# Raw expert weights loaded into the place of their f16 parts, and the expert's number loaded first in the expert step

## The reference

```
xn = layernorm(x)
x  = x + differential_attention(xn) + moe(xn)

def moe(xt):                       # 8 experts, 2 of them for each token, and a shared expert for all
    logits = xt @ gate_w.T
    idx    = top_k(logits + beta, 2);  probs = sigmoid(logits[idx])
    h      = silu(xt @ gate_proj_w[e]) * (xt @ up_proj_w[e])       # 256 -> 512
    out    = sum over the token's two experts of probs * (h @ down_proj_w[e])
    return out + shared_expert(xt)
```

## Time and profile before

| | us |
|---|---|
| median of 3 runs | 3512.49 (3509.45 to 3520.72) |
| the profiled execution, whole | 3520.69 |
| its span in the profile | 3518.9 |
| TensorE busy in the span | 3220.9 (92%) |
| VectorE busy | 2810.6 (80%) |
| ScalarE busy | 2318.1 (66%) |
| POOL busy | 1648.7 (47%) |

### The profile page before, as it was taken

How to read it: one execution, slowest core, us unless ns; L and a number is a source line. 1 busy time by engine, 2 the same in 40 slices (tenths; PEclk the granted TensorE clock), 3 DMA queues, 4 the chain that set the end, 5 groups by cost and what they waited for, 6 DMA issues and landing times. The chain is left out here.

```text
span 3518.9 us, 61065 instructions
## 1 busy us (share of the span) xinstructions
PE 3220.9 (92%) x19800; PEld 1295.5 (37%) x19815; DVE 2810.6 (80%) x4905; ACT 2318.1 (66%) x3660; POOL 1648.7 (47%) x2104
## 2 busy tenths in 40 slices
PE   6777789999999999999999999868999999999987
PEld 3434456663222222222222222252333333333333
DVE  5564643468999999999999999476888999889997
ACT  3342333335888888788888878856767767777763
POOL 1331340002444444434344444405777888888885
PEclk9887899998999999999999999988999999999998
DMA  3233221111111111111111111041222222222221
GB/s 126 95 102 97 99 74 55 54 49 44 31 50 39 39 38 36 35 35 35 35 32 34 30 30 31 17 156 52 70 72 65 75 82 70 73 81 69 73 75 52
DMA packets 160888, 211.62 MB, mean 60 GB/s; under 512 B 32324, under 2 KB 108364, under 8 KB 160604
## 3 DMA queue, kind: packets, MB, share of 16 engines
q1 hardware_dynamic: 141340, 172.51, 16.4%
q0 software_dynamic: 8512, 18.76, 1.7%
q10 hardware_dynamic: 10752, 16.78, 1.4%
HBM read 154.48 MB, written 52.69 MB: 59 GB/s over the span
## 5 line engine op out<-in xcount | busy, mean ns | idle before, releaser
L1408 ACT ACTIVATE prob<-psS 128x1024 f32<-128x1024 f32 (+3 forms) x1280 | 1104.4, 906 | 278.9 <-PE psS L1592 269.4
L1458 DVE TENSOR_REDUCE pmax<-psR 128x1 f32<-128x512 f32 x1674 | 1057.0, 684 | 78.4 <-PE psR L1534 46.6
L2234 POOL TENSOR_TENSOR hc<-h_d,crep 128x512 f32<-128x512 f32 x512 | 646.9, 1271 | 189.8 <-DVE h_d L2463 139.6
L1534 PE MATMUL psR<-kslab,qslab 48*128 48x512 bf16 (+3 forms) x2480 | 652.5, 351 | 22.4 <-DVE pmax L1458 14.0
L1607 PE MATMUL psVo<-prob,vaug 128*32 128x512 f32 (+3 forms) x5120 | 629.8, 546 | 1.3 <-ACT ov L1412 0.6
L1592 PE MATMUL psS<-qslab,kslab 51*128 51x512 bf16 (+3 forms) x2560 | 533.3, 354 | 39.9 <-ACT prob L1408 23.0
L2463 DVE TENSOR_TENSOR_SCAN h_d<-a,state,psU 128x512 f32<-128x512 f32 x384 | 489.3, 1275 | 0.0
L1323 POOL TENSOR_SCALAR_AFFINE_SELECT prob<-prob 128x256 f32<-128x256 f32 (+1 forms) x512 | 213.4, 420 | 533.1 <-ACT prob L1408 533.1
L2453 DVE TENSOR_TENSOR psU<-dtx,psX 128x512 f32<-128x512 f32 x512 | 356.2, 696 | 92.7 <-PE psX L2613 42.8
L1534 PEld LDWEIGHTS psR<-kslab,qslab 48*128 48x128 bf16 x2480 | 187.2, 94 | 629.0 <-DVE pmax L1458 478.6
L2366 ACT ACTIVATE a<-dt,a_neg 128x512 f32<-128x512 f32 x512 | 366.9, 724 | 54.1 <-DVE h_d L2463 53.2
(11 more groups left out here) (347 smaller groups left out, 5260.8 us busy)
## 6 DMA issues: line engine op xcount, KB each, us to landing
crep<-c_rows_d SPq DMA_DIRECT2D x256, 256.0 KB, 3.1
x_e<-rows_d SPq DMA_DIRECT2D x72, 128.0 KB, 2.0
y_d<-y SPq DMA_DIRECT2D x72, 128.0 KB, 1.7
q_d<-parts SPq DMA_DIRECT2D x48, 128.0 KB, 2.3
k_d<-parts SPq DMA_DIRECT2D x48, 128.0 KB, 2.3
qslab<-q_d SPq DMA_DIRECT2D x60, 96.0 KB
kslab<-k_d SPq DMA_DIRECT2D x60, 96.0 KB
raw_w<-n_L_ffn_gate_proj_w_dram ACTq DMA_DIRECT2D x8, 512.0 KB, 3.8
```

Of the source, the lines that this page charges most:

```text
L1408: act.activation(prob[g % BUFS][:, :, off:BLK], psS[g % 2][:, :, off:BLK], ACT.Exp).then_inc(prob_ready, 1)
L1458: dve.tensor_reduce(into[:, lo:lo + (count - 1) * NEXT + 1:NEXT], psR[at % BANKS][:, 0:count * w].rearrange("p (n w) -> p n w", w=w), AX.X ...
L1534: ins = pe.matmul(dst[:, m * w:(m + 1) * w], qslab[u][rows, i * P:(i + 1) * P], kslab[u][rows, ch * BLK:ch * BLK + w], start=(m == 0), sto ...
L2234: pool.tensor_tensor(hc[:, g % CR], h[:, g % HR], crep[:, g // PAIR % SPR], ALU.mult).then_inc(hc_ready, 1)
```

## The change

Front: the two f16 parts of a matrix of one expert now lie side by side (`wg`, `wu`, `wd` in place of six tensors `wgh` to `wdl`), which is as much room as the raw f32 matrix needs, and the raw matrix is loaded there. Scaling goes from there to a buffer `scaled_w` (the size of the old `raw_w`, for one expert), the high part is a copy of it in f16 over the raw values, and POOL subtracts from the same buffer. Each f16 copy now signals, and each subtraction waits for its own copy; each scaling waits for the last expert's subtraction of the same matrix. The load of expert 1 is issued ahead of ScalarE's block 0, and at the end of block n that of expert n+2. The six ScalarE operations of a block lie in another order. The maximum is three operations of 1024 instead of one of 3072. Expert step on TensorE: the `value_load` of the expert's number comes first, ahead of the transposes of h; the transposes of the next tile's x lie between G and U (for tile 0 they stay ahead of all).

```diff
--- before.py
+++ after.py
@@ -151,8 +151,10 @@
         gate_rows = hT[0:E, 0, 0:D]
         y = sg[:].rearrange("p s (j d) -> p (s j) d", d=D)
         wsg, wsu, wsd = sb("wsg", [P, KD, M]), sb("wsu", [P, KD, M]), sb("wsd", [P, M // P, D])
-        raw = sb("raw_w", [P, 3, KD * M])
-        zeros = raw[:, 0, 0:D]
+        scaled = sb("scaled_w", [P, 3, KD * M])
+        zeros = scaled[:, 0, 0:D]
+        raw = [keep[name][:].rearrange("p e x m -> p (e x m)").bitcast(F32).rearrange("p (e m) -> p e m", e=E)
+               for name in ("wg", "wu", "wd")]
         wmax = sb("wmax", [P, 3])
         wmax_r = sb("wmax_r", [3, 1])
         diag_r = sb("diag_r", [3, 3])
@@ -198,7 +200,7 @@
         raw_in = sem("a_raw_in")
         wscale_step = sem("a_wscale_step")
         wmax_moved = sem("a_wmax_moved")
-        whigh_ready = sem("a_whigh_ready")
+        wsplit_step = sem("a_wsplit_step")
         wlow_ready = sem("a_wlow_ready")
 
         block = ctx.enter_context(nc.Block())
@@ -269,11 +271,10 @@
         def _(pool):
 
             def low_weights(e):
-                for w, low in enumerate((keep["wgl"], keep["wul"], keep["wdl"])):
-                    high = (keep["wgh"], keep["wuh"], keep["wdh"])[w]
-                    pool.wait_ge(whigh_ready, 3 * e + w + 1 + CREDIT)
-                    pool.tensor_tensor(low[:, e].rearrange("p k m -> p (k m)"), raw[:, w],
-                                       high[:, e].rearrange("p k m -> p (k m)"), ALU.subtract).then_inc(wlow_ready, 1)
+                for w, name in enumerate(("wg", "wu", "wd")):
+                    pool.wait_ge(wsplit_step, 6 * e + 2 * w + 2 + CREDIT)
+                    pool.tensor_tensor(keep[name][:, e, 1], scaled[:, w], keep[name][:, e, 0], ALU.subtract)\
+                        .then_inc(wlow_ready, 1)
 
             c = Chain(pool, pchain)
             c.after(pool.memset(keep["ident"][:], 0.0))
@@ -394,7 +395,9 @@
             def weight_max(e):
 
                 dve.wait_ge(raw_in, 48 * e + 48 + CREDIT)
-                dve.tensor_reduce(wmax[:], raw[:], AX.X, ALU.max, apply_absolute_value=True).then_inc(wscale_step, 1)
+                for w in range(3):
+                    ins = dve.tensor_reduce(wmax[:, w:w + 1], raw[w][:, e], AX.X, ALU.max, apply_absolute_value=True)
+                ins.then_inc(wscale_step, 1)
 
             def weight_row(e):
                 dve.wait_ge(wmax_moved, 2 * e + 1 + CREDIT)
@@ -481,20 +484,23 @@
         def _(act):
 
             def load_expert(e):
-                act.wait_ge(wlow_ready, 3 * e + CREDIT)
+                act.wait_ge(raw_in, 48 * e + CREDIT)
                 for w, (name, rows) in enumerate((("gate_proj", KD), ("up_proj", KD), ("down_proj", M // P))):
-                    act.dma_start(raw[:, w].rearrange("p (k m) -> p k m", k=rows),
+                    act.dma_start(raw[w][:, e].rearrange("p (k m) -> p k m", k=rows),
                                   io[name][e].rearrange("(k p) m -> p k m", p=P)).then_inc(raw_in, 16)
 
+            def scaled_weights(e, w):
+
+                act.wait_ge(wscale_step, 3 * e + 3 + CREDIT)
+                if e:
+                    act.wait_ge(wlow_ready, 3 * e - 2 + w + CREDIT)
+                act.activation(scaled[:, w], raw[w][:, e], ACT.Copy, scale=keep["wscale"][:, w, e:e + 1])\
+                   .then_inc(wsplit_step, 1)
+
             def high_weights(e, w):
 
-                act.wait_ge(wscale_step, 3 * e + 3 + CREDIT)
-                high = (keep["wgh"], keep["wuh"], keep["wdh"])[w]
-                act.activation(high[:, e].rearrange("p k m -> p (k m)"), raw[:, w], ACT.Copy,
-                               scale=keep["wscale"][:, w, e:e + 1])
-
-            def scaled_weights(e, w):
-                act.activation(raw[:, w], raw[:, w], ACT.Copy, scale=keep["wscale"][:, w, e:e + 1]).then_inc(whigh_ready, 1)
+                act.wait_ge(wsplit_step, 6 * e + 2 * w + 1 + CREDIT)
+                act.copy(keep[("wg", "wu", "wd")[w]][:, e, 0], scaled[:, w]).then_inc(wsplit_step, 1)
 
             load_expert(0)
             act.wait_ge(gate_t, 1 + CREDIT)
@@ -548,30 +554,31 @@
 
             token_root(0)
             copy_turned(0)
+            load_expert(1)
             for n in range(NBLK):
                 scores(n)
                 copy_rows(n, 0)
                 copy_rows(n, 1)
                 gate(n, 0)
                 gate(n, 1)
-                high_weights(n, 0)
                 scaled_weights(n, 0)
                 if n + 1 < NBLK:
                     token_root(n + 1)
                 copy_rows(n, 2)
+                high_weights(n, 0)
+                scaled_weights(n, 1)
+                copy_rows(n, 3)
+                gate(n, 2)
                 high_weights(n, 1)
-                copy_rows(n, 3)
-                scaled_weights(n, 1)
-                gate(n, 2)
+                scaled_weights(n, 2)
+                gate(n, 3)
                 high_weights(n, 2)
-                gate(n, 3)
-                scaled_weights(n, 2)
                 if n + 1 < NBLK:
                     copy_turned(n + 1)
                 copy_shared(n)
                 copy_values(n)
-                if n + 1 < NBLK:
-                    load_expert(n + 1)
+                if n + 2 < NBLK:
+                    load_expert(n + 2)
             assert E == NBLK
 
         @block.tensor
@@ -1006,8 +1013,10 @@
                 return pe.matmul(dst, low, w_high, start=False, stop=last)
 
             def step(i, s):
-                if known(i + 1, 0):
+                if isinstance(i, int) and i < 0:
                     turn_x(i + 1, 1 - s)
+                if known(i, 0):
+                    e = pe.value_load(at(keep["table"][0:1, 0], i), min_val=0, max_val=E - 1)
                 if known(i - 1, 0):
                     pe.wait_ge(h_ready, i + CREDIT)
                     if known(i - 1, 1):
@@ -1016,14 +1025,15 @@
                         ins = pe.transpose(psH[:, m], h[:, 1 - s, m * P:(m + 1) * P], keep["ident"][:])
                     ins.then_inc(h_turned, 1)
                 if known(i, 0):
-                    e = pe.value_load(at(keep["table"][0:1, 0], i), min_val=0, max_val=E - 1)
                     pe.wait_ge(xTl_ready, i + 1 + CREDIT)
                     for w, dst, done in (("wg", psG, g_done), ("wu", psU, u_done)):
                         if dst is psU:
+                            if known(i + 1, 0):
+                                turn_x(i + 1, 1 - s)
                             max_product(i, 0)
                         for k in range(KD):
-                            w_high, w_low = (keep[w + part][:, bass.ds(e, 1), k].rearrange("p o m -> p (o m)")
-                                             for part in "hl")
+                            w_high, w_low = (keep[w][:, bass.ds(e, 1), part, k * M:(k + 1) * M].rearrange("p o m -> p (o m)")
+                                             for part in range(2))
                             ins = split_products(dst[:], xTh[:, s, k], xTl[:, s, k], w_high, w_low, k == 0, k == KD - 1)
                         ins.then_inc(done, 1)
                 max_product(i, 1)
@@ -1033,8 +1043,8 @@
                     if known(i - 1, 1):
                         pe.wait_ge(y_ready, i - 1 + CREDIT)
                     for m in range(MT):
-                        w_high, w_low = (keep["wd" + part][:, bass.ds(e, 1), m].rearrange("p o d -> p (o d)")
-                                         for part in "hl")
+                        w_high, w_low = (keep["wd"][:, bass.ds(e, 1), part, m * D:(m + 1) * D].rearrange("p o d -> p (o d)")
+                                         for part in range(2))
                         ins = split_products(psY[:], hTh[:, 1 - s, m], hTl[:, 1 - s, m], w_high, w_low, m == 0, m == MT - 1)
                     ins.then_inc(d_done, 1)
                 max_product(i, 2)
@@ -2692,10 +2702,8 @@
                 keep["hot"] = sb(moe, "hot_all", [P, NBLK, 2, TPB, E])
                 keep["slot"] = sb(moe, "slot_all", [P, NBLK, 2 * TPB])
                 keep["table"] = sb(moe, "table", [P, 2, RT], I32)
-                for part in "hl":
-                    keep["wg" + part] = sb(moe, "wg" + part, [P, E, KD, M], F16)
-                    keep["wu" + part] = sb(moe, "wu" + part, [P, E, KD, M], F16)
-                    keep["wd" + part] = sb(moe, "wd" + part, [P, E, M // P, D], F16)
+                for name in ("wg", "wu", "wd"):
+                    keep[name] = sb(moe, name, [P, E, 2, KD * M], F16)
                 keep["wmag"] = sb(moe, "wmag", [P, 3, E])
                 keep["wscale"] = sb(moe, "wscale", [P, 3, E])
                 keep["onehot"] = sb(moe, "onehot", [P, E, RT])
```

## The result

The changed kernel takes 3489.63 us (median of 5 runs, 3486.59 to 3494.36) against 3512.49 us (5 runs, 3509.45 to 3521.97): ratio 0.9928, 95% interval 0.9909 to 0.9947. It is faster, by 23 us and not by 53.5, and 13.6 us above the upper end of the forecast range.

The account below looks back on a forecast made before the run. It took a cycle of waits on late raw weights to bound the front, and TensorE the expert stage. 47.8 + 0.4 + 1.3 + 4.0 = 53.5 us off 3512.5 gave 3459.0 us, range 3447 to 3476.

Parts of the forecast that it names:

- Early load: Front: raw weights arrive a block earlier, so `choose` starts 6.83 us sooner in each of seven blocks, 47.8 us gained.
- What is late next: Front, TensorE: about 1.5 us of the old wait returns at `spread_max`, taking nothing from the 47.8 us.
- rival 1: Front: TensorE's clock falls in the idle time at `spread_max`, costing 12 us in 7 blocks; time 3471, chance 0.11.
- The split on ScalarE, POOL's run: Front: reordered ScalarE operations, up to 1.1 us later, are covered and POOL's subtractions stay unbroken; no cost.
- The loads' queue: Front, ScalarE's DMA queue: block 7's table load no longer stands behind the issuing of a weight load; 0.4 us gained.
- rival 4: Front: a gap in POOL's subtractions lets VectorE in, up to 4 us a block gained; time 3427, chance 0.03.
- rival 5: Front: raw data early, but `choose` still 3 us late or more; half the gain 3483, none 3512; chance 0.04.
- First expert step: Start of the expert stage: G of tile 0 now precedes X of tile 1, gaining 1.3 us.
- Expert loop: Expert steps: the number's load hides behind the D products; 4 us gained, bounds -7 to +5.9.
- Rival 3: Expert step, ScalarE's order: a late X delays sg and h, TensorE waits every step; 3535 us, slower, chance 0.02.
- rival 2: Expert step: h comes later than D's end, 72 x 0.15 = 11 us lost instead of 4 gained; 3474, chance 0.08.
- the fit of 0.08 for h: Expert steps, loop and late: h, wanted 0.22 us sooner under the new order, would still be ready with 0.08 to spare.

Follow-up runs that it names:

- e8: e1 with the raw weights of expert n+1 loaded at the end of block n again, as in the kernel before; 3518.87 us, ratio 1.0006.
- e1: The changed kernel with both edits of the expert step taken back, keeping the new front and weight layout; 3473.33 us, ratio 0.9874.
- e5: The changed kernel, but ScalarE copies y of tile i-2 ahead of the cast of the next x; 3466.97 us, ratio 0.9852.
- e2: The kernel before with only the new order of the expert step (number first, X between G and U); 3534.28 us, ratio 1.0058.
- e3: The changed kernel with the load of the expert's number back behind the transposes of h; 3487.19 us, ratio 0.9917.
- e10: e3 with ScalarE's copy of y moved ahead of the cast of the next x; 3484.62 us, ratio 0.9903.
- e4: The changed kernel with the transposes of x back at the head of the step, behind the number's load; 3469.36 us, ratio 0.9872.
- e6: e1 with the load of the expert's number, behind the transposes of h, done twice; 3513.0 us, ratio 0.9985.
- e7: e1 with POOL's three subtractions of each block waiting for VectorE's last hidden product; 3406.17 us, ratio 0.9685.

## Why the prediction was right in the front and wrong in the expert stage

- *Early load* (47.8 us): right in mechanism and size; `choose` of block 7 is 48.3 us sooner, its blocks 46.6 us apart as forecast (46.7), and e8 shows that nothing else brings it. Two of the seven profiled runs with this front (e1, e5) give 45.
- *What is late next*: 1.5 us forecast at `spread_max`, 2.0 measured, and it takes nothing from the gain. u0 behind it runs 1.98 us, full clock: rival 1 falls.
- *The split on ScalarE, POOL's run*: at nothing, rightly (e8 against before: 1.0006).
- *The loads' queue* (0.4): the 0.50 us ahead of block 7's table load are gone.
- *Rivals 4 and 5*: the hold (6.86 us in block 4 before, 7.28 after) wasn't broken up: rival 4 falls, and so does rival 5, since `choose` starts 0.10 us behind the sigmoid.
- *First expert step* (1.3): the first G won 1.5, but nothing of it was left at the first transposes of h. The forecast let only one transposition run at half clock; the granted clock of 0.50 held through G and nearly all of U. The term is 0.
- *Expert loop* (+4, bounds -7 to +5.9): this is the step that failed. Measured -19.3 in the loop and -2.9 behind it. The lower bound of 0.1 us a step was no bound; e2 gives the order's price by itself, 18 us more than before.

Where that step went wrong: it compared when data are ready with when they are wanted, for h, sg and y, and all of that came out nearly as worked out. h ends at 512.01, right where D ends; y is ready before D. What it left out is that an instruction stream also has to get past its waits ahead of the products. It had y's copy end about 2.4 us behind G's start (measured 2.36), but used that only for sg, the next in ScalarE's queue. It never set it against D, which waits for y and starts 2.8 behind G, only 0.44 after the copy. At the same time it counted on the number's load to "run while the twelve D products are still in TensorE's queue". The late copy took away what the load needs: y first brings back 0.55 us a step (e5). Rival 3 named the right place, ScalarE's order in the expert step behind the moved X, but the wrong victim: it is not sg and h that come late but y, and rival 2, with h as the cause, had the nearest price (0.15 a step, measured 0.45 in the loop). Neither was the mechanism.

A second error lay under it. "TensorE is the bound: 59.94 of 60 us busy at clock 1.00", with "Only what shortens its own chain counts there", hid that the step of 4.69 us can also be read as a chain through VectorE's h and the load. The Trainium skill ("Perfetto Trace Analysis", section "Identifying the Most-Contended Engine") says that the share of busy matmul time is no good measure of how close TensorE is to its best, because pipelined instructions look smaller in the trace. The rows agree that it misleads, but here it is too large: the records of G and U are 0.38 us long and 0.215 apart, and by the starts of its products TensorE had 4.56 us of work in 4.69 (97%) where the view has 99.9% busy. e3 and e10 add no product and lengthen the step by 0.35 to 0.39.

With y first, the prediction's picture of the loop holds (e5: mean 4.59, forecast 4.56 to 4.65), and the time against its own reference is 50.4 us less, against 53.5 forecast. In the late steps, with the maxima between, the number first costs 0.11 to 0.12 us a step (e5 5.57, e4 5.58, e1 5.46). It is not the fit of 0.08 for h that failed there: in late steps of e5 h ends 0.18 to 0.47 us ahead of its transposes. What does cost is not shown.

## What to carry to other kernels

For each wait that stands ahead of a long run of products, ask not only whether the data are there when the products are due, but how far ahead of them the wait is passed: a load or register work that is to hide behind those products needs that lead. Before moving work from one end of a step to the middle, follow every engine that serves it to the next item in its own queue, to y here, which has nothing to do with the moved transposes. And an engine that looks full in busy time need not be the bound by its products alone: a run that adds something outside them, such as one suspected cost doubled (e6), tells whether that cost is hidden.

## What the runs showed of the hardware

- A second load of one number from memory into a register of TensorE, behind the first, lengthened the loop steps by 0.64 us, the late ones by 0.62, and the two written-out steps ahead of the loop by 0.53 and 0.57 (5.09 and 5.12 against 4.56 and 4.55; e6 against e1). With the load ahead of the transposes of h and X behind G, a step took 4.59 or 5.14 us, by the place of a copy on another engine.
- A wait ahead of D that ended 0.44 us before D's first product (510.44 against 510.88) and one that ended 1.67 us before it (497.64 against 499.31 in e5) went with loop steps of 5.14 and 4.59 us, though the data were there in both. At 0.44 the next transposes came 0.38 and 1.00 us behind h in turn.
- VectorE was held through all three of POOL's subtractions again, 7.28 us for an operation that takes 0.69 in e7, and that hold was worth more than the change: 67 us (e7 against e1). The profile has VectorE's operation start 0.44 us ahead of POOL's first. At this place the Trainium skill ("SBUF — State Buffer", section "SBUF: two separate sides") has the side that starts first keep the shared pair of ports for one whole instruction; the rows show a longer hold, and of an operation whose recorded start is the earlier one. The same section names as those that need the pair VectorE's operations with two inputs from that memory or in a mode that uses two ports; the maximum has one input, and in e7 it runs 1.21 us from 199.18, beside a subtraction from 199.35, just as long as without one (1.21 at 238.91).
- TensorE, idle for 2.0 us, went on at full clock (u0 1.98 us); idle for 6.98 it came back at a granted clock of 0.50 (the 1.2 GHz level), which held until 244.3 us, for the first 5 us of `down`: 9.75 us instead of 7.17, which ran at 1.00 throughout (e7).
